# A four-block attention and expert kernel: PSUM banks drawn from rings of seven, and the second attention's output projection and denominators in bf16 parts

## The reference

```python
x = x + tanh(g_xattn[0]) * L0_xattn(layernorm(x), ctx)   # 16 heads of 16, 1585 keys and 16 separate ones
x = x + tanh(g_ffn[0])   * L0_ffn(layernorm(x))          # 16 experts of width 128 on 64 latents, top 8, one shared
x = x + tanh(g_xattn[1]) * L1_xattn(layernorm(x), ctx)   # 16 heads of 128, 1601 keys:
#   q = x Wq ; k = ctx Wk ; v = ctx Wv (8 key/value heads, each for two query heads)
#   out = softmax(q k^T / sqrt(128), masked) v ; result = out Wo
x = x + tanh(g_ffn[1])   * L1_ffn(layernorm(x))          # ternary weights, silu gate, width 1024
```

## Time and profile before

| | before |
|---|---|
| median of 3 runs | 1485.71 us (1482.29 to 1487.23) |
| profiled execution | 1487.37 us, its span 1486.1 us |
| TensorE / VectorE / ScalarE / GpSimd busy | 91% / 69% / 60% / 46% of the span |
| mean granted TensorE clock | 0.96 |
| matmul records | 8524 |

### The profile page before, as it was taken

One profiled execution on the slowest core, in us unless ns is written; L12 is line 12 of the kernel. 1 busy time (PEld: TensorE's weight loads), 2 busy tenths in 40 slices (PEclk: granted clock), 3 DMA queues, 4 the chain that ended last, 5 costly groups with the idle time before them and its releaser, 6 DMA issues.

```text
span 1486.1 us, 24911 instructions
## 1 busy us (share of the span) xinstructions
PE 1356.2 (91%) x8524; PEld 675.7 (45%) x8524; DVE 1025.3 (69%) x2259; ACT 894.9 (60%) x1575; POOL 680.9 (46%) x753
## 2 busy tenths in 40 slices
PE   5688979889878988789999999999999999999998
PEld 4243434334333344335455545545454555454555
DVE  5677787687787256756766666756667776767656
ACT  4656657557655756366665666555665555656554
POOL 4035343243040023157655547565576565555553
PEclk8799989999989999889999999999999999999999
DMA  4000301201250100001000000000010000000000
GB/s 174 1 1 15 77 2 24 46 1 28 42 199 1 58 0 6 23 23 29 1 1 1 23 1 24 6 1 23 1 29 29 1 30 1 30 1 1 1 2 29
DMA packets 20484, 36.66 MB, mean 25 GB/s; under 512 B 4898, under 2 KB 15238, under 8 KB 19334
## 3 DMA queue, kind: packets, MB, share of 16 engines
q1 hardware_dynamic: 20358, 35.07, 8.1%
HBM read 26.53 MB, written 1.15 MB: 19 GB/s over the span
## 4 chain that ended last, share of the span: by engine, by line
PE 50%; issue 3%; DVE 2%; ACT 2%; POOL 2%; DVEq 0%; POOLq 0%; ACTq 0%
PE BK L732 50%; POOL arena L2141 1%; DVE arena L1696 1%; DVE arena L2330 0%; ACT arena L1981 0%; ACT arena L1993 0%; DVE arena L2336 0%; POOL arena L1104 0%; PE BK L1377 0%; ACT L1024 0%; PE BK L1051 0%; ACT arena L2362 0%; ACT arena L2366 0%; POOL arena L2132 0%; POOL arena L1102 0%
## 5 line engine op out<-in xcount | busy, mean ns | idle before, releaser
L732 PE MATMUL BK<-arena 128*128 128x512 bf16 (+13 forms) x8194 | 1314.9, 365 | 94.5 <-DVE arena L1533 17.2
L732 PEld LDWEIGHTS BK<-arena 128*128 128x128 bf16 (+7 forms) x8194 | 639.9, 110 | 737.8 <-issue 193.2
L2141 POOL TENSOR_TENSOR arena<-arena 128x512 bf16<-128x512 f32 (+1 forms) x416 | 440.0, 1062 | 244.5 <-ACT arena L1981 187.0
L1981 ACT ACTIVATE arena<-BK,arena 128x512 f32<-128x512 f32 (+1 forms) x416 | 285.7, 687 | 199.0 <-PE BK L732 193.8
L1879 ACT ACTIVATE arena<-BK 128x512 f32<-128x512 f32 (+1 forms) x416 | 222.8, 601 | 116.7 <-PE BK L732 114.4
L1533 DVE TENSOR_REDUCE arena<-BK 128x1 f32<-128x512 f32 x384 | 241.3, 683 | 59.0 <-PE BK L732 58.4
L1721 DVE TENSOR_TENSOR BK<-BK,arena 128x512 f32<-128x512 f32 (+1 forms) x352 | 244.3, 694 | 44.8 <-ACT arena L1981 41.0
L1696 DVE CUSTOM_DVE_ANT_0 arena<-BK,arena 128x512 bf16<-128x512 f32 (+1 forms) x256 | 147.2, 575 | 109.7 <-PE BK L732 106.8
L1993 ACT ACTIVATE arena<-BK 128x512 bf16<-128x512 f32 (+1 forms) x256 | 129.9, 507 | 104.6 <-PE BK L732 104.6
L1735 DVE SCALAR_TENSOR_TENSOR arena<-BK,arena 128x256 f32<-128x256 f32 x128 | 56.1, 480 | 34.8 <-PE BK L732 34.7
L2044 POOL TENSOR_TENSOR arena<-arena 128x1024 f32<-128x1024 f32 (+2 forms) x15 | 23.3, 1550 | 86.4 <-DVE arena L1475 86.4
(11 more groups left out here) (184 smaller groups left out, 841.8 us busy)
## 6 DMA issues: line engine op xcount, KB each, us to landing
arena<-arena SPq DMA_DIRECT2D x144, 50.0 KB, 2.2
arena<-in_ctxT SPq DMA_DIRECT2D x8, 800.5 KB, 4.4
arena<-in_ctxk SPq DMA_DIRECT2D x4, 768.0 KB
arena<-in_wo SPq DMA_DIRECT2D x1, 2048.0 KB, 7.9
arena<-in_wqT SPq DMA_DIRECT2D x1, 2048.0 KB, 8.9
arena<-in_x SPq DMA_DIRECT2D x4, 256.0 KB, 9.7
arena<-in_rsel SPq DMA_DIRECT2D x1, 1024.0 KB, 9.4
arena<-in_rw1T SPq DMA_DIRECT2D x1, 1024.0 KB, 5.3
```

Of the source, the lines that this page charges most:

```text
L732: return T.matmul(out_, lhsT, rhs, start=start, stop=stop, skip_group_check=True)
L1981: A.activation(P1[k][0:m, :], BK[i][0:m, :], ACT.Exp, scale=SCALE1, bias=mcb[0:m, b, kt:kt + 1]).then_inc(free[i], 1)
L2141: G.tensor_tensor(Pl[k][0:m, :], P1[k][0:m, :], Ph[k][0:m, :], ALU.subtract).then_inc(p_low, 1)
```

## The change

Two things. First, banks: oB, oC, oD and the norm's transposes (all but turn 0 of batch 0, turn 2 from batch 2 on, and turn 3), the routing, the folds, the `up` results, the tails and the maxima of the first two pairs of heads take the next bank of a ring of seven (`self.turn`) where a bank was named. In `stage0` that is the ring in use already, in `stage1` a ring of 0, 1, 2, 3, 4, 5, 7. In the engines' code BK[7] becomes BK[i] for them. Second, block three: N1, the values that o1p reads and the sums that o1a reads are held as two bf16 parts each. o1p becomes three bf16 products (high x high, high x low, low x high), o1a two. ScalarE's copies write the high parts; two new VectorE steps, o1w and o1t, write the low ones; N1 is split on GpSimd by two more steps per fold. In order, o1t stands at the end of the second tile of the next pair of heads, and o1w one tile after o1a. The diff, cut:

```diff
-        self.fill(7, "ln", turn, b)
+        self.fill(next(self.turn) if 0 < 4 * turn + b < 10 else 7, "ln", turn, b)
...
         def finish(g):
             piece("oA", g)
             yield
-            piece("oB", g, bank=7)
+            piece("oB", g, bank=next(self.turn))
             yield
             if g % 4 == 3:
-                piece("oC", g // 4, bank=7)
-                yield
-                piece("oD", g // 4, bank=7)
+                piece("oC", g // 4, bank=next(self.turn))
+                yield
+                piece("oD", g // 4, bank=next(self.turn))
                 yield
                 yield from self.norm(to, 1, g // 4)
 
+        self.turn = mbank
...
-            yield from routed(to, 0, 3)
+            yield from routed(to, 0, mbank)
 
         def routed(to, ch, bank):
             for k in (2, 1, 0):
-                self.fill(bank, "x2", ch, k)
+                self.fill(next(bank), "x2", ch, k)
                 to.append(("x2", ch, k))
                 yield
                 if k == 2:
-                    self.fill(bank, "rt", ch)
+                    self.fill(next(bank), "rt", ch)
                     to.append(("rt", ch))
...
-            self.fill(bank, "wt", ch)
+            self.fill(next(bank), "wt", ch)
...
-                piece("fold", h, bank=7)
+                piece("fold", h, bank=next(self.turn))
...
-        def tail(ch, banks):
+        def tail(ch):
             for i in range(4):
-                piece("tl", ch, i, bank=banks[i])
-                yield
-
-        ends = chain(self.last, self.routed(to, 1, 7))
+                piece("tl", ch, i, bank=next(self.turn))
+                yield
+
+        self.turn = itertools.cycle((0, 1, 2, 3, 4, 5, 7))
+        ends = chain(self.last, self.routed(to, 1, self.turn))
         work = chain(fold(), context())
         def values():
...
-                    self.fill(3 * (s % 2) + k, "up", s, k)
+                    self.fill(next(self.turn), "up", s, k)
...
-                    ends = chain(tail(0, [7] * 4), self.norm(to, 2, 0), self.norm(to, 2, 1))
+                    ends = chain(tail(0), self.norm(to, 2, 0), self.norm(to, 2, 1))
...
-        for _ in tail(1, [0, 1, 2, 3]):
+        for _ in tail(1):
             next(ahead, None)
         piece("vl", 0)
         piece("mcl")
         for _ in ahead:
             pass
         piece("mcb")
+        self.ended = self.fills[:]
 
...
-                self.fill(4, "md", g, k // 2, k % 2)
+                self.fill(next(self.turn) if g < 2 else 4, "md", g, k // 2, k % 2)
...
-                self.fill(5, "mb", g, (k - 1) // 2, (k - 1) % 2)
+                self.fill(next(self.turn) if g < 2 else 5, "mb", g, (k - 1) // 2, (k - 1) % 2)
...
+        self.turn = itertools.cycle((4, 5))
...
             piece("o1v", g)
             piece("o1a", g, bank=7)
             yield
+            piece("o1w", g)
             yield
...
             pace(2)
+            if kt == 1 and s > NKT:
+                piece("o1t", g - 1)
...
+        n1s = sb("n1s", [128, 256], F32, F0)
...
-        N1 = sb("N1", [128, H, D], F32, Region(q_end - 16 * KB, q_end))
+        N1h, N1l = (sb(f"N1{i}", [128, H, D], BF16, Region(q_end - 16 * KB + 8 * KB * i, q_end - 8 * KB + 8 * KB * i))
+                    for i in range(2))
...
-        acc = sb("acc", [128, 2, 512], F32, L1)
-        oN = sb("oN", [128, H, S], F32, L1)
+        acch, accl = (sb(f"acc{i}", [128, 2, 512], BF16, L1) for i in range(2))
+        oNh, oNl = (sb(f"oN{i}", [128, H, S], BF16, L1) for i in range(2))
...
                     if kt == 0:
                         pe.wait_ge(pv_taken, g - 1)
+                        pe.wait_ge(free[j], plan.ended[j])
...
                     for u in range(4):
-                        t = mm(BK[7][:, u:u + 1], acc[:, g % 2, 128 * u:128 * u + 128], ones[:, 0:1])
+                        mm(BK[7][:, u:u + 1], acch[:, g % 2, 128 * u:128 * u + 128], onb[:, 0:1], stop=False)
+                        t = mm(BK[7][:, u:u + 1], accl[:, g % 2, 128 * u:128 * u + 128], onb[:, 0:1], start=False)
...
+                    pe.wait_ge(n1_split, H)
                     for t2 in range(2):
-                        t = mm(BK[i][:, 256 * t2:256 * t2 + 256], oN[:, h, 128 * t2:128 * t2 + 128], N1[:, h, :])
+                        o, tok = BK[i][:, 256 * t2:256 * t2 + 256], slice(128 * t2, 128 * t2 + 128)
+                        mm(o, oNh[:, h, tok], N1h[:, h, :], stop=False)
+                        mm(o, oNh[:, h, tok], N1l[:, h, :], start=False, stop=False)
+                        t = mm(o, oNl[:, h, tok], N1h[:, h, :], start=False)
...
+                elif kind == "o1w":
+                    g, = arg
+                    h, j = 2 * (g % 8), 2 + g % 2
+                    dve.wait_ge(pv_high, g + 1)
+                    V.tensor_tensor(oNl[:, h:h + 2, :].rearrange("p h n -> p (h n)"), BK[j][:, :],
+                                    oNh[:, h:h + 2, :].rearrange("p h n -> p (h n)"), ALU.subtract).then_inc(pv_taken, 1)
+                elif kind == "o1t":
+                    g, = arg
+                    dve.wait_ge(acc_high, g + 1)
+                    if g >= 2:
+                        dve.wait_ge(*filled("o1a", g - 2))
+                    V.tensor_tensor(accl[:, g % 2, :], BK[6][:, :], acch[:, g % 2, :], ALU.subtract).then_inc(acc_out, 1)
...
-                    A.copy(m1s[:, :], BK[7][:, 0:256]).then_inc(m1_staged, 1)
-                    A.copy(N1[:, h, :], BK[7][:, 256:512]).then_inc(free[7], 1)
+                    A.copy(m1s[:, :], BK[i][:, 0:256]).then_inc(m1_staged, 1)
+                    if h:
+                        act.wait_ge(n1_split, h)
+                    A.copy(n1s[:, :], BK[i][:, 256:512]).then_inc(free[i], 1)
...
-                    A.copy(oN[:, h:h + 2, :].rearrange("p h n -> p (h n)"), BK[j][:, :]).then_inc(pv_taken, 1)
+                    A.copy(oNh[:, h:h + 2, :].rearrange("p h n -> p (h n)"), BK[j][:, :]).then_inc(pv_high, 1)
...
-                    A.copy(acc[:, g % 2, :], BK[6][:, :]).then_inc(acc_out, 1)
+                    A.copy(acch[:, g % 2, :], BK[6][:, :]).then_inc(acc_high, 1)
...
+                    pool.wait_ge(*emptied("fold", h))
+                    G.tensor_copy(N1h[:, h, :], n1s[:, :]).then_inc(pool_chain.sem, pool_chain.up())
+                    pool.wait_ge(pool_chain.sem, pool_chain.n)
+                    G.tensor_tensor(N1l[:, h, :], n1s[:, :], N1h[:, h, :], ALU.subtract).then_inc(n1_split, 1)
```

## The result

The changed kernel takes 1444.91 us (median of 4 runs, 1443.74 to 1452.4), the kernel before 1484.14 us beside it (4 runs, 1482.29 to 1487.23). The ratio is 0.974, between 0.971 and 0.978, which is some 38 us. Where this text gives what a run saved, it is one minus the ratio, times the time of the kernel before beside it; the medians can differ from that by 2 us. The profiled execution took 1444.05 us with a span of 1442.7, against a forecast of 1444.3.

The account below looks back on a forecast made before the run. TensorE was taken to bound the second attention (772.6 of 787 us busy), with waits mattering before it. -13.3 - 17.3 + 4 - 6 - 5.5 - 5 = -43.1 us, from 1487.4 to 1444.3, about 1443 us at the median; range 1421 to 1464.

Parts of the forecast that it names:

- Part 1: Second attention: o1p in bf16 instead of fp32 takes 0.41 us less per pair of heads, 32 times, -13.3 us.
- Part 2: Second attention: o1a in bf16 pairs takes 0.54 us less per pair of heads, -17.3 us (+1.6 to -19.2).
- Rival D: Second attention: bf16 one-column matmuls at 0.109 us, no gain from o1a, waits of 0.3 us; about 1484 us, chance 0.03.
- Part 3: Second attention: VectorE's new steps o1w and o1t add 0.12 us of wait per pair of heads, +4 us (0 to +16).
- Part 4, the first attention: oB, oD and norms on the ring end waits for bank 7 there, less than half returning: -6 us (0 to -13.5).
- Part 4, the experts: Pieces sharing bank 7 in the experts move to the ring; most waits come back, -5.5 us (0 to -6.8).
- Part 4, the first maxima: Second attention's first maxima: seven banks let TensorE stay ahead; half the idle time returns, -5 us (0 to -9.9).
- Part 5: Folds: splitting N1 on GpSimd costs nothing, or at most 1 us each where folds follow closely.
- A: Rings give almost nothing outside the maxima, new VectorE steps cost 0.3 us per pair of heads; about 1460 us, chance 0.20.
- B: Whole kernel: everything comes back and no wait is added, -62.7 us; about 1423 us, chance 0.12.
- C: Second attention: o1w late in every pair of heads, no gain from rings, +35 us; about 1521 us, chance 0.03.

Follow-up runs that it names:

- pool_waits: The changed kernel plus one wait on GpSimd, so its subtraction for the third tile comes behind VectorE's first sum; 1437.58 us, ratio 0.967.
- rings_only: The changed kernel with every bf16 part undone, leaving only the new banks; 1470.7 us, ratio 0.987 to the kernel before.
- change_again: The changed kernel run once more without an edit; 1446.51 us, ratio 0.971 to the kernel before.
- bf16_only: The changed kernel with the banks of the kernel before, keeping the bf16 parts; 1465.79 us, ratio 0.984 to the kernel before.

## Why the prediction came out as it did

The total was right, 1443 against 1444.9, and so were the signs of all terms. That it was right to 2 us is luck. The first attention gave more than forecast, by 4 us as timed and 6.6 in the profile, o1a 2.2 us more, and the new VectorE steps took back 4 to 6 us more. Part of what the stages gained isn't waiting at all but the same matmuls at a higher granted clock, which the prediction doesn't name.

- **Part 1, o1p, -13.3 us.** 55.3 to 42.0 us of TensorE's time: -13.3. A price from the same shape in the same stage is as good as a measurement.
- **Part 2, o1a, -17.3 us.** 0.61 us a pair, -19.5 for 32 (-18.3 in the sum, with the wait behind the last one in it). I chose 0.035 us a load, near mt's 0.03; it was 0.025 in the pair shown (8 in 0.20 us). Taking the value near the closest row and not the middle of the bounds was right. The fp32 loads took 0.102 us each, so the bf16 form is four times as fast. The Trainium skill, "TensorE: Matmul & The Clock Gate", section "Weight-path perf modes — Fast Weight Load (FWL) and DoubleRow", has about 2x as measured, by which the 32 pairs would have taken an estimated 6.5 us more than they did; here the measurement decides. What is compared here is fp32 with bf16, so that mode's own factor isn't shown. Rival D is gone with it.
- **Part 3, the new VectorE steps, +4 us (0 to +16).** The price in the stage is 10.0 us at like clocks (8.4 in the first profile), inside the bounds, and it is the term that I got wrong, for two reasons. I looked at o1w as the step that o1p might wait for; a wait of o1p for it stands in the trace once, 1.1 us, at the kernel's end. And I wrote of o1t that "only 0.68 us is new", as if the instruction behind it kept its own length. It doubled, because it was pushed beside GpSimd's subtraction. 7.4 of the 10.0 us went with pool_waits. The Trainium skill, "SBUF — State Buffer", section "Who interferes with whom", has the rule that the price of this term needed: VectorE and GpSimd share a port pair as an exclusive lock, and "SBUF: two separate sides" adds that a VectorE instruction with two SBUF inputs takes it against a GpSimd instruction that reads SBUF. By that rule, the trace agrees: the first sum is held, GpSimd is held where the sum came first, and the 352 later sums with one input in PSUM take 700 ns at most. The question to ask of a step put into a queue is not only what waits behind it, but what each of those will then run beside.
- **Part 4, the first attention, -6 us (0 to -13.5).** About -10 by timing. I took less than half of the 13.5 us because VectorE would be what TensorE waits for next. It was: the maxima's wait grew by 6.9 us and the last maximum's by 4.7. As a term of waiting the forecast was good, some 6 us of idle time over 13 profiles and 8.0 in this pair. The rest is TensorE's busy time, 4.5 us in this pair at a granted clock of 0.94 against 0.93, and it moves by 12 us between profiles of the same banks. The share that each freed piece had stays open.
- **Part 4, the experts, -5.5 us (0 to -6.8).** -4.3, and -5.1 in rings_only. The waits for bank 7 went, all 6.8 us; a norm's wait, now 3.3 us, took back some.
- **Part 4, the first maxima, -5 us (0 to -9.9).** -3.6, but not as waiting: TensorE's idle time rose by 1.3 us, and the 4.9 us less of busy time came with the clock at 0.96 instead of 0.84. change_again has -5.3, with the idle time of before, 7.0 us. Here the number came near and the mechanism was wrong. My sign for it, under 24 us where it had been 29, wasn't met either: 29 less 3.6 is 25.4. ScalarE's readers became the limit, as I had named them.
- **Part 5, the fold's split, 0.** bf16_only, which has the split and not the rings, takes 79.1 us for the experts where before took 78.6. Half a microsecond in one profile can't be told from nothing.
- **The rivals.** A said that the rings give almost nothing outside the maxima. rings_only refutes it with 18.7 us. B said that all comes back; the waits above say no. C said that o1w would be late in every pair. It was late once.

## What to carry to other kernels

When an instruction is put into one engine's queue, find what the instructions behind it will now overlap with on the other engines, and compare their inputs: a VectorE instruction with both inputs in SBUF is held while GpSimd reads SBUF, and a wait on the engine that has slack can be the repair. Before a shorter stage is put down to a wait that went, compare TensorE's busy and idle time and the granted clock in both. A buffer taken out of turn from a ring makes the next owner of that buffer wait, even where most others are free; before giving it another one, look which engine last reads that one. To test such an order, change the order for the others and leave the suspected piece alone: that control showed what a plain before and after could not.

## What the runs showed of the hardware

- A fp32 tensor_tensor of 128x512 from SBUF, 0.70 us when free, took 1.57 us when GpSimd's subtraction (1.04 us) had started 0.03 us ahead of it: it ended 0.56 us after GpSimd's, as 30 of the 32 did, so it ran mostly after it. With the overlap taken away (pool_waits) the median was 701 ns. The same shape with one input in PSUM took 0.70 us beside GpSimd.
- Who starts first holds the other: a sum begun 0.06 us ahead of GpSimd's subtraction took 0.70 us, and the subtraction 1.53 us in place of 1.04.
- Bf16 matmuls of one column with a full load each follow at 0.025 us, where fp32 ones followed at 0.10 us.
- The first attention took 413.4 to 422.3 us in ten profiles with the same banks. Its idle time moved by 4.3 us, its busy time by 12.5, with the granted clock between 0.95 and 0.90. At a granted clock of 1.00 a stage repeats: 741.7 us for the second attention in three profiles with the wait on GpSimd. The same stage of the change was 747.5 and 749.1 us, and the difference is one piece at 1.2 GHz, in a window where TensorE was busy for 17.5 of 20 us in both.
